# Summing each token's chosen key and value head as a GpSimd tree over a double buffer, in place of a strided VectorE sum

## The chip, the cores and the metric

The kernel runs on one core of a Trainium2 chip. The metric is the device time in microseconds (us) of one execution, lower is better. TensorE (PE in the rows) multiplies matrices into PSUM, VectorE (DVE) and ScalarE (ACT) read PSUM and SBUF, GpSimd (POOL) works on SBUF, and SyncE (SP) issues most of the transfers. All engines run their own list of instructions in order and meet only at semaphores.

## The reference, cut to what matters

The input is one sequence of 2048 tokens of width 256. Three layers follow each other: an attention layer, a gated recurrence, and the attention layer again with the same weights. In an attention layer each token has 16 query heads of 16 elements, but it picks only one of its 16 key heads and one of its 16 value heads:

```python
gating = softmax(x @ W_gate.T)                       # 16 gates per token
indicator = one_hot(argmax(gating), H)
gating_top1 = indicator * max(gating)
qkv = x @ W_qkv.T
k_shared = einsum('bth,bthd->btd', indicator, k)     # the chosen key head, 16 wide
v_shared = einsum('bth,bthd->btd', gating_top1, v)   # the chosen value head, scaled
att = softmax(causal(q @ k_shared.T / sqrt(hd)))
y = att @ v_shared
```

`k_shared` and `v_shared` are sums over the 16 heads, of which all but one are multiplied by zero. These two sums are what the change is about.

## The kernel before, in words

The tokens are four chunks of 512 (`c`), each of four tiles of 128 tokens (`t`). The attention of a layer `l` (0 and 1), a chunk and a group of four heads is a unit, 32 in all. For a unit the kernel first computes all scores once to find the row maxima ("max": a PSUM bank of TensorE scores at L1116, reduced by VectorE at L930, or, for the diagonal blocks, copied by ScalarE at L807, masked by GpSimd at L623 and reduced by VectorE at L936), then computes the scores again ("qk": L1139 and L1142), takes the exponential on ScalarE (L816), masks diagonal blocks on GpSimd (L608, two per diagonal step), and multiplies with the values ("pv": L1152).

Before a chunk's attention comes its preparation, `prepare(l, c)`, of which there are eight: statistics, normalisation, transposes, queries ("q"), gates ("gate", "pick"), and for each of the four tiles "kv" and "choose". "kv" is a TensorE product of all 16 key and 16 value heads into one PSUM bank (L1054), and a VectorE multiplication of that bank with the pick weights into `prod`, 512 elements per token (L894). "choose" is one VectorE reduction over the 16 heads, which reads `prod` with a stride of 16 elements and writes 32 elements of `kv` (L903). VectorE then waits for its own result before its next instruction. "kpack" takes all four tiles of `kv` on ScalarE (L766 and behind), GpSimd computes the rest of the key (L638, L644), ScalarE copies it, and "keys" transposes them on TensorE (L1067). GpSimd also splits the queries (L632, "split"), adds the attention's output to `x_sb` (L614, "fin"), and works in the statistics (L587 to L599) and the recurrence (L653 to L683).

The order of the instructions on every engine is one list, `ORDER`, made by a planner on the host, `weave()` (L155). It keeps a planned time for each engine, takes the duration of each piece from the table `WEIGHT` (L121), and picks among scores, sums, maxima and the side work (preparations and recurrence, whose start is set by `SIDE_WORK`, L111) the one that would be free to start first. In each step the maxima are ranked by how far VectorE's planned time lies ahead. Side work other than "kv", "q" and "skip" is placed behind the planned end of the side work before it (`side_end`). The first preparation, (0,0), stands at the front of the list with no other work beside it. The planner knows of GpSimd's time, but a "pv" behind a diagonal mask is planned at a fixed 900 ns after its scores, however busy GpSimd is.

The PSUM banks of the maxima, preparations and recurrence are a ring of three; TensorE waits before filling a bank until its reader has freed it.

Of the kernel before, what the change touches and what calls it, by code (L numbers as in the profile page):

```python
# [6 lines left out]
D = 256  # L7
H = 16
HD = D // H
S = 128  # L10
P = 128
# [91 lines left out]
def branch(c):  # L103
# [18 lines left out]
    "weights": (300, [("ACT", 400)]), "wgate": (150, [("ACT", 200)]), "bias": (400, [("DVE", 200)]),  # L122
    "stats": (0, [("DVE", 2200), ("POOL", 1500)]), "norm": (0, [("ACT", 2300)]), "turn": (800, [("ACT", 600)]),
    "gate": (2800, [("DVE", 500), ("ACT", 250)]), "pick": (0, [("DVE", 1500)]),
    "kv": (1900, [("DVE", 690)]), "choose": (0, [("DVE", 1020)]), "q": (1900, [("ACT", 600), ("DVE", 690)]),
    "split": (0, [("ACT", 650), ("POOL", 1200)]), "qout": (0, []), "qin": (0, []),
    "kpack": (0, [("ACT", 900), ("POOL", 350)]), "krest": (0, [("ACT", 350), ("POOL", 350)]),
    "keys": (500, [("ACT", 1000)]), "gates": (1900, [("ACT", 690)]), "scan": (0, [("DVE", 1300), ("POOL", 1300)]),
# [187 lines left out]
def macaron_block(nc, x, gamma, beta, w_in, b_in, w_out, b_out, w_skip, b_skip, w_gate, w_qkv, out):  # L316
# [6 lines left out]
    with ctx:  # L323
        def sb(name, shape, dt=f32):
            return ctx.enter_context(nc.sbuf_tensor(name, shape, dt))
# [48 lines left out]
        cand = sb("cand", [P, TC, H])  # L374
        cmx = sb("cmx", [P, TC])
        pick = sb("pick", [P, TC, 2, H])
        prod = sb("prod", [P, 2 * D])
        kv = sb("kv", [P, TC, 2 * HD])

        k_rest = sb("k_rest", [P, TC, HD])  # L380
# [171 lines left out]
        def _(pool):  # L552
# [64 lines left out]
            def diagonal(e):  # L617

                n = DIAG_NO[e]
                if n % 2:  # L620
                    pool.wait_ge(s_ra, FREED[e])
                    d = diag_pair(n // 2)
                    g_.affine_select(out=d, in_=d, compare_op=ALU.is_ge, fill=LOWEST, base=0,  # L623
                                     pattern=[[0, 2 * GH], [-1, P]], channel_multiplier=1).then_inc(s_dm, 1)

            def preparation(e):
                kind, l, c = e[0], e[1], e[2]
                n = prep_no(l, c)
                if kind == "split":
                    b = e[3]  # L630
                    pool.wait_ge(s_q2, NO[e] + 1)
                    g_.tensor_tensor(q_part[:, 2, b, :], q_rest[:, b, :], q_part[:, 1, b, :],  # L632
                                     op=ALU.subtract).then_inc(s_q3, 1)
                elif kind == "kpack":
                    pool.wait_ge(s_k1, n + 1)
                    if n:
                        pool.wait_ge(s_krow, n)
                    g_.tensor_tensor(k_rest[:, :, :], kv[:, :, 0:HD], k_rows[:, 0, :, 0:HD], op=ALU.subtract)\  # L638
                        .then_inc(s_kr, 1)
                elif kind == "krest":  # L640
                    pool.wait_ge(s_kr, n + 1)
                    pool.wait_ge(s_k2, n + 1)
                    rows = k_rows[:, 1, :, :].rearrange("p t (o r) -> p t o r", o=2)[:, :, :, HD:2 * HD]
                    g_.tensor_tensor(rows, k_rest[:, :, :].unsqueeze(2).to_broadcast([P, TC, 2, HD]),  # L644
                                     k_rows[:, 0, :, HD:2 * HD].unsqueeze(2).to_broadcast([P, TC, 2, HD]),
                                     op=ALU.subtract).then_inc(s_krow, 1)
# [38 lines left out]
            for e in ORDER:  # L685
                if e[0] in ("qk", "fin"):
                    attention(e)
                elif e[0] == "stats":
                    stats_of(e)
                    if NO[e] == 0:  # L690
                        constants()
                elif on_diagonal(e):
                    diagonal(e)
                elif e[0] in ("split", "kpack", "krest"):
                    preparation(e)
                elif e[0] in ("bias", "scan", "add") or (e[0] == "norm" and e[1] == 2) \
                        or (e[0] == "gates" and e[2] == 0):
                    recurrence(e)

        @block.scalar  # L700
        def _(act):
# [40 lines left out]
            def preparation(e):  # L742
                kind, l, c = e[0], e[1], e[2]
                n = prep_no(l, c)
                if kind == "gate":
                    act.wait_ge(s_rd, FREED[e])
                    a_.activation(ge[:, :, :], gd[:, :, :], ACT.Exp).then_inc(s_ge, 1)
                elif kind == "q":
                    b = e[3]
                    act.wait_ge(s_fill, filled(e))  # L750
                    if n:
                        act.wait_ge(s_qw[b], 16 * n)
                    a_.activation(q_part[:, 0, b, :], bank_of(e)[:, :], ACT.Copy).then_inc(s_q1, 1)  # L753
                elif kind == "split":
                    b = e[3]
                    act.wait_ge(s_rd, FREED["q", l, c, b])
                    a_.activation(q_part[:, 1, b, :], q_rest[:, b, :], ACT.Copy).then_inc(s_q2, 1)
                elif kind == "kpack":
                    act.wait_ge(s_kv, n + 1)
                    if n == 0:  # L760
                        act.wait_ge(s_const, 1)
                    else:

                        act.wait_ge(s_fill, filled(RING_USERS[max(RING_NO[p] for p in RING_NO
                                                                  if p[0] == "keys" and NO[p] == n - 1)]))
                    a_.activation(v_l[:, l, TC * c:TC * c + TC, 0:HD], kv[:, :, HD:2 * HD], ACT.Copy)  # L766
                    rows = k_rows[:, 1, :, :].rearrange("p t (o r) -> p t o r", o=2)[:, :, :, 0:HD]
                    a_.activation(rows, kv[:, :, 0:HD].unsqueeze(2).to_broadcast([P, TC, 2, HD]), ACT.Copy)
                    rows = k_rows[:, 0, :, :].rearrange("p t (g a d) -> p t g a d", g=4, a=2)
                    a_.activation(rows[:, :, :, 0, :], kv[:, :, 0:HD].unsqueeze(2).to_broadcast([P, TC, 4, HD]),  # L770
                                  ACT.Copy).then_inc(s_k1, 1)
                elif kind == "krest":
                    act.wait_ge(s_kr, n + 1)
                    rows = k_rows[:, 0, :, :].rearrange("p t (g a d) -> p t g a d", g=4, a=2)
                    a_.activation(rows[:, :, :, 1, :], k_rest[:, :, :].unsqueeze(2).to_broadcast([P, TC, 4, HD]),
                                  ACT.Copy).then_inc(s_k2, 1)
# [61 lines left out]
        def _(dve):  # L838
# [3 lines left out]
            def own(ins):  # L842
                n_own[0] += 1
                ins.then_inc(s_dch, 1)
                dve.wait_ge(s_dch, n_own[0])
# [19 lines left out]
            def preparation(e):  # L865
# [24 lines left out]
                elif kind == "kv":  # L890
                    t = e[3]
                    dve.wait_ge(s_fill, filled(e))
                    w = pick[:, t, :, :].rearrange("p a h -> p (a h)")
                    v_.tensor_tensor(prod[:, :].rearrange("p (g d) -> p g d", d=HD),  # L894
                                     bank_of(e)[:, :].rearrange("p (g d) -> p g d", d=HD),
                                     w.unsqueeze(2).to_broadcast([P, 2 * H, HD]), op=ALU.mult)\
                        .then_inc(s_rd, 1)
                elif kind == "choose":
                    t = e[3]
                    dve.wait_ge(s_rd, FREED["kv", l, c, t])  # L900
                    if n and t == 0:
                        dve.wait_ge(s_krow, n)
                    last = v_.tensor_reduce(kv[:, t, :].rearrange("p (a d) -> p a d", a=2),  # L903
                                            prod[:, :].rearrange("p (a h d) -> p a d h", a=2, h=H),
                                            axis=AX, op=ALU.add)
                    if t < TC - 1:
                        own(last)
                    else:
                        last.then_inc(s_kv, 1)
                        dve.wait_ge(s_kv, n + 1)  # L910
                elif kind == "q":
                    b = e[3]
                    dve.wait_ge(s_q1, NO[e] + 1)
                    if n:

                        dve.wait_ge(s_q3, NO[e] - 1)
                    v_.tensor_tensor(q_rest[:, b, :], bank_of(e)[:, :], q_part[:, 0, b, :],  # L917
                                     op=ALU.subtract).then_inc(s_rd, 1)
# [75 lines left out]
            for e in ORDER:  # L994
                if e[0] in ("fold", "join") or (e[0] == "max" and not on_diagonal(e)):
                    maxima(e)
                elif e[0] == "fin":
                    finish(e)
                elif e[0] == "stats":
                    stats_of(e)  # L1000
                elif e[0] in ("gate", "pick", "kv", "choose", "q"):
                    preparation(e)
                elif e[0] in ("bias", "scan", "rec") or (e[0] == "gates" and e[2] == 1):
                    recurrence(e)
# [191 lines left out]
```

## Time and profile before

| what | value |
|---|---|
| median of three runs | 1118.13 us (1112.92 to 1118.16) |
| the profiled execution | 1121.33 us |
| its span, first to last instruction | 1119.6 us |
| mean granted TensorE clock | 0.926 of full speed |
| VectorE busy | 812.9 us, 73% of the span |
| GpSimd busy | 284.8 us, 25% of the span |

The span is what the profile shows instruction by instruction; the time of an execution has 1.7 us around it. Busy time of TensorE is modelled at its end, so that a high share of it does not mean that TensorE works at its peak. A line of a group of instructions gives the line in the kernel, the engine, the operation, the tile written and the tiles read, the shapes, and the count.

### The profile page before, as it was taken

How to read it: one execution, taken by the hardware profiler on the slowest of the kernel's cores; microseconds unless marked ns; L12 is line 12 of the kernel's file. 1: busy time of each engine (PE TensorE's matmuls, PEld its weight loads, DVE VectorE, ACT ScalarE, POOL GpSimd, SP SyncE). 2: the span in 40 equal slices, each digit the busy share in tenths (PEclk: the TensorE clock that was granted, in tenths of full speed). 3: DMA queues.
4: the chain of work that ended last, by engine and by line, in shares of the span. 5: the costliest groups of instructions: out<-in, count | busy, mean ns of one | idle time of the engine just before them, and what ended most of it. 6: DMA issues, size and time to landing. Idle time of an engine off the chain costs nothing.

```text
span 1119.6 us, 20056 instructions
## 1 busy us (share of the span) xinstructions
PE 1027.9 (92%) x7762; PEld 385.0 (34%) x7762; DVE 812.9 (73%) x1441; ACT 713.9 (64%) x1016; POOL 284.8 (25%) x511
## 2 busy tenths in 40 slices
PE   8697898898998997899998999999999999999997
PEld 5334333333233332233333433333333333332322
DVE  3565668778586897679594777886768899999630
ACT  3354357845666674667466754875757777787786
POOL 2244212313223113121113312234222111210314
PEclk8687889998899997899798997998999999999999
DMA  5202011011001100000110011000002000000001
GB/s 161 66 16 71 6 53 29 2 57 30 1 1 43 44 1 1 1 1 1 43 44 1 1 57 30 2 2 19 1 15 71 2 1 20 2 2 1 3 3 38
DMA packets 29966, 26.48 MB, mean 24 GB/s; under 512 B 5664, under 2 KB 29872, under 8 KB 29872
## 3 DMA queue, kind: packets, MB, share of 16 engines
q1 hardware_dynamic: 29056, 24.40, 7.2%
q8 instruction: 62, 1.02, 0.4%
q10 hardware_dynamic: 816, 0.80, 0.2%
q14 instruction: 32, 0.26, 0.1%
HBM read 16.54 MB, written 8.39 MB: 22 GB/s over the span
## 4 chain that ended last, share of the span: by engine, by line
PE 58%; DVE 19%; ACT 8%; issue 4%; POOL 3%; DMA 0%; SPq 0%; POOLq 0%; DVEq 0%; ACTq 0%
PE ps_o L1152 17%; DVE mxp L930 14%; PE ps_x L1116 12%; PE ps_s L1139 8%; PE ps_s L1142 7%; ACT probs L816 4%; PE ps_x L1054 3%; PE ps_x L1059 2%; PE ps_x L1085 2%; PE ps_x L1092 1%; PE ps_x L1125 1%; DVE mxp L936 1%; PE ps_x L1038 1%; PE ps_x L1049 1%; ACT d_sb L807 1%
## 5 line engine op out<-in xcount | busy, mean ns | idle before, releaser
L930 DVE TENSOR_REDUCE mxp<-ps_x 128x1 f32<-128x512 f32 (+2 forms) x960 | 600.1, 682 | 131.5 <-PE ps_x L1116 129.9
L816 ACT ACTIVATE probs<-ps_s 128x1024 f32<-128x1024 f32 (+3 forms) x640 | 545.0, 896 | 222.2 <-PE ps_s L1142 219.6
L1116 PE MATMUL ps_x<-k_tl,q_t 64*128 64x512 bf16 (+2 forms) x1792 | 337.9, 314 | 23.0 <-DVE mxp L930 10.4
L1152 PE MATMUL ps_o<-probs,v_l 128*32 128x512 f32 (+3 forms) x2560 | 310.2, 561 | 9.0 <-POOL probs L608 8.5
L1139 PE MATMUL ps_s<-q_t,k_tl 64*128 64x512 bf16 (+3 forms) x1280 | 288.4, 363 | 13.2 <-ACT probs L816 11.8
L1142 PE MATMUL ps_s<-q_t,k_tl 34*128 34x512 bf16 (+3 forms) x1280 | 286.9, 361 | 0.0
L1116 PEld LDWEIGHTS ps_x<-k_tl,q_t 64*128 64x128 bf16 x1792 | 112.2, 98 | 332.1 <-DVE mxp L930 212.8
L608 POOL TENSOR_SCALAR_AFFINE_SELECT probs<-probs 128x256 f32<-128x256 f32 x256 | 102.2, 407 | 232.6 <-ACT probs L816 229.8
L623 POOL TENSOR_SCALAR_AFFINE_SELECT d_sb<-d_sb 128x1024 f32<-128x1024 f32 x64 | 69.4, 1092 | 260.4 <-ACT d_sb L807 244.3
L1139 PEld LDWEIGHTS ps_s<-q_t,k_tl 64*128 64x128 bf16 x1280 | 81.1, 96 | 110.0 <-ACT probs L816 77.6
L1142 PEld LDWEIGHTS ps_s<-q_t,k_tl 34*128 34x128 bf16 x1280 | 95.5, 97 | 42.1 <-issue 5.4
L807 ACT ACTIVATE d_sb<-ps_x 128x512 f32<-128x512 f32 x128 | 70.6, 606 | 28.7 <-PE ps_x L1116 26.6
L1152 PEld LDWEIGHTS ps_o<-probs,v_l 128*32 128x32 f32 x2560 | 52.3, 109 | 98.0 <-issue 79.7
L936 DVE TENSOR_REDUCE mxp<-d_sb 128x8 f32<-128x1024 f32 x64 | 77.4, 1209 | 0.9 <-POOL d_sb L623 0.9
L1054 PE MATMUL ps_x<-wqkv_t,ut 128*128 128x512 f32 x128 | 63.9, 625 | 1.1 <-DVE prod L894 0.5
L917 DVE TENSOR_TENSOR q_rest<-ps_x,q_part 128x512 f32<-128x512 f32 x16 | 11.1, 691 | 62.9 <-ACT q_part L753 62.9
L614 POOL TENSOR_TENSOR x_sb<-x_sb,y_att 128x256 f32<-128x256 f32 x32 | 24.1, 755 | 95.7 <-DVE y_att L962 95.5
L1059 PE MATMUL ps_x<-ut,wqkv_t 128*128 128x512 f32 x64 | 38.7, 736 | 8.5 <-ACT ut L731 8.5
L958 DVE RECIPROCAL rec<-ps_x 128x16 f32<-128x16 f32 x32 | 8.1, 253 | 45.9 <-PE ps_x L1125 45.8
L753 ACT ACTIVATE q_part<-ps_x 128x512 bf16<-128x512 f32 x16 | 9.6, 597 | 48.4 <-PE ps_x L1059 48.4
L894 DVE TENSOR_TENSOR prod<-ps_x,pick 128x512 f32<-128x512 f32 x32 | 22.1, 691 | 23.5 <-PE ps_x L1054 22.9
L823 ACT ACTIVATE o_sb<-ps_o 128x512 f32<-128x512 f32 x32 | 19.2, 601 | 21.6 <-PE ps_o L1152 21.6
(100 smaller groups left out, 558.5 us busy)
## 6 DMA issues: line engine op xcount, KB each, us to landing
q_t<-q_scratch SPq DMA_DIRECT2D x192, 64.0 KB, 2.2
q_scratch<-q_part SPq DMA_DIRECT2D x16, 384.0 KB, 2.5
x_sb<-in_L_attn_x_dram SPq DMA_DIRECT2D x4, 512.0 KB, 8.3
out_dram<-x_sb SPq DMA_DIRECT2D x4, 512.0 KB, 2.9
q_t<-m_row SPq DMA_DIRECT2D x64, 4.0 KB
wqkv_n<-in_L_ffn_W_qkv_dram ACTq DMA_DIRECT2D x1, 768.0 KB, 6.7
w_in_sb<-in_L_attn_W_in_dram SPq DMA_DIRECT2D x1, 384.0 KB, 5.7
w_skip_sb<-in_L_attn_W_skip_dram SPq DMA_DIRECT2D x1, 256.0 KB, 5.2
```

The source lines that it names most:

```text
L608: g_.affine_select(out=pr, in_=pr, compare_op=ALU.is_ge, fill=0.0, base=0, pattern=[[0, 2], [1, P]], channel_multiplier=-1).then_inc(s_msk, 1)
L623: g_.affine_select(out=d, in_=d, compare_op=ALU.is_ge, fill=LOWEST, base=0, pattern=[[0, 2 * GH], [-1, P]], channel_multiplier=1).then_inc ...
L807: a_.activation(d_sb[:, n % DIAG_BUFS, :], bank_of(e)[:, :], ACT.Copy).then_inc(s_ra, 1)
L816: a_.activation(probs[:, s % NB, 2 * hp:2 * hp + 2, P * i:QW], ps_s[hp][:, :, P * i:QW], ACT.Exp, scale=SCALE).then_inc(s_exp, 1)
L930: v_.tensor_reduce(mxp[:, heads[0] % 2, h0:h1, tiles[0]:tiles[-1] + 1:i_step, slot], bank_of(e)[:, :].rearrange("p (h i k) -> p h i k", i= ...
L936: v_.tensor_reduce(mxp[:, :, :, 2 * i2:2 * i2 + 2, 2].rearrange("p o h i -> p (o h) i"), diag_pair(2 * v + i2).rearrange("p (x i) k -> p x ...
L1054: last = mm(bank[:, :], ut[:, dc, t * P:(t + 1) * P], wqkv_t[:, dc, D:3 * D], start=dc == 0, stop=dc == DC - 1)
L1059: last = mm(bank[:, :], wqkv_t[:, dc, b * P:(b + 1) * P], ut[:, dc, :], start=dc == 0, stop=dc == DC - 1)
L1116: last = mm(bank[:, col:col + w], q_rows(0, ROWS_A, c, g, hh, i * P, P), k_cols(0, ROWS_A, hh, l, key // P, w), start=True, stop=True)
L1139: mm(ps_s[hp][:, hh, P * i:QW], k_cols(0, ROWS_A, hh, l, kt, P), q_rows(0, ROWS_A, c, g, 2 * hp + hh, P * i, QW - P * i), start=True, stop ...
L1142: last = mm(ps_s[hp][:, hh, P * i:QW], k_cols(1, ROWS_B, hh, l, kt, P), q_rows(1, ROWS_B, c, g, 2 * hp + hh, P * i, QW - P * i), start=Fal ...
L1152: last = mm(ps_o[VW * hh:VW * hh + VW, P * i:QW], v_l[:, l, kt, :], probs[:, s % NB, hh, P * i:QW], start=j == 0, stop=j == key_tiles(c) - 1)
```

## The change

"choose" moves from VectorE to GpSimd. There it is a tree of four additions in place: 8 heads onto 8, 4 onto 4, 2 onto 2, and the last into `kv`, each for key and value together (256, 128, 64 and 32 elements per partition). The first three each wait for their own end before the next. `prod` becomes two buffers, by the parity of the tile. VectorE's multiplication now waits until the "choose" two before it has ended (`s_kv` counts every "choose" now, not every fourth), and ScalarE's "kpack" waits for all four. The reduction, and VectorE's waits around it, are gone. In the planner's table "choose" goes from 1020 ns on VectorE to 1900 ns on GpSimd, so `ORDER` is planned anew from there.

```diff
-    "kv": (1900, [("DVE", 690)]), "choose": (0, [("DVE", 1020)]), "q": (1900, [("ACT", 600), ("DVE", 690)]),
+    "kv": (1900, [("DVE", 690)]), "choose": (0, [("POOL", 1900)]), "q": (1900, [("ACT", 600), ("DVE", 690)]),
...
-        prod = sb("prod", [P, 2 * D])
+        prod = sb("prod", [P, 2, 2 * D])
...
+            def choose(e):
+                _, l, c, t = e
+                n = prep_no(l, c)
+                pool.wait_ge(s_rd, FREED["kv", l, c, t])
+                if n and t == 0:
+                    pool.wait_ge(s_krow, n)
+                parts = prod[:, t % 2, :].rearrange("p (a h d) -> p a h d", a=2, h=H)
+                w = H // 2
+                while w > 1:
+                    own(g_.tensor_tensor(parts[:, :, 0:w, :], parts[:, :, 0:w, :], parts[:, :, w:2 * w, :], op=ALU.add))
+                    w //= 2
+                g_.tensor_tensor(kv[:, t, :].rearrange("p (a d) -> p a d", a=2), parts[:, :, 0, :], parts[:, :, 1, :],
+                                 op=ALU.add).then_inc(s_kv, 1)
...
-                    act.wait_ge(s_kv, n + 1)
+                    act.wait_ge(s_kv, TC * (n + 1))
...
-                    v_.tensor_tensor(prod[:, :].rearrange("p (g d) -> p g d", d=HD),
+                    if NO[e] >= 2:
+                        dve.wait_ge(s_kv, NO[e] - 1)
+                    v_.tensor_tensor(prod[:, t % 2, :].rearrange("p (g d) -> p g d", d=HD),
...
-                elif kind == "choose":
-                    t = e[3]
-                    dve.wait_ge(s_rd, FREED["kv", l, c, t])
-                    if n and t == 0:
-                        dve.wait_ge(s_krow, n)
-                    last = v_.tensor_reduce(kv[:, t, :].rearrange("p (a d) -> p a d", a=2),
-                                            prod[:, :].rearrange("p (a h d) -> p a d h", a=2, h=H),
-                                            axis=AX, op=ALU.add)
-                    if t < TC - 1:
-                        own(last)
-                    else:
-                        last.then_inc(s_kv, 1)
-                        dve.wait_ge(s_kv, n + 1)
```

## Rows read from the trace of the kernel before

**Rows 1.** The page: busy time by engine (part 1), the chain by engine (part 4)
```profile
PE 1027.9 (92%) x7762; PEld 385.0 (34%) x7762; DVE 812.9 (73%) x1441; ACT 713.9 (64%) x1016; POOL 284.8 (25%) x511
...
PE 58%; DVE 19%; ACT 8%; issue 4%; POOL 3%; DMA 0%; SPq 0%; POOLq 0%; DVEq 0%; ACTq 0%
```

**Rows 2.** Waits of all engines: total us, times, longest
```profile
PEld ps_x L1116 <- DVE mxp L930: 212.8, 415, 1.6
...
PE ps_o L1152 <- POOL probs L608: 8.5, 4, 4.7
```

**Rows 3.** Groups by form, VectorE: busy us, mean ns, idle before, releasers
```profile
L930 DVE TENSOR_REDUCE mxp<-ps_x 128x1 f32<-128x512 f32 x768 | 478.0, 681 | 68.9 <-PE ps_x L1116 67.6
...
L903 DVE TENSOR_REDUCE kv<-prod 128x32 f32<-128x512 f32 x32 | 32.4, 1013 | 0.3
L894 DVE TENSOR_TENSOR prod<-ps_x,pick 128x512 f32<-128x512 f32 x32 | 22.1, 691 | 23.5 <-PE ps_x L1054 22.9
```

**Rows 4.** The chain, shares by line, in 232:262, 354:384, 554:580, 652:678, 826:856
```profile
by line: PE ps_x L1054 19.5%; PE ps_o L1152 13.2%; DVE mxp L930 12.3%; PE ps_x L1116 11.3%; DVE prod L894 5.9%; PE ps_x L1059 5.7%; DMA q_t<-m_row 5.7%; PE ps_s L1142 5.1%; PE ps_s L1139 5.1%; DVE kv L903 3.4%; issue 2.9%; PE ps_x L1125 2.1
...
by line: DVE mxp L930 32.8%; DVE kv L903 13.0%; PE ps_x L1054 12.8%; DVE prod L894 6.9%; PE ps_o L1152 6.6%; PE ps_x L1059 5.8%; PE ps_s L1139 5.5%; issue 5.3%; PE ps_s L1142 4.9%; PE ps_x L1116 4.7%; ACT q_part L753 2.0%; DVE rec L958 0.9%
...
by line: PE ps_x L1054 33.5%; PE ps_o L1152 20.5%; PE ps_x L1116 15.1%; PE ps_s L1139 9.0%; PE ps_s L1142 8.5%; PE ps_x L1059 6.6%; ACT probs L816 6.3%; DVE prod L894 2.7%; issue 1.9%; DVEq L892 0.1%
...
by line: PE ps_x L1054 29.6%; PE ps_o L1152 20.8%; PE ps_x L1116 11.1%; PE ps_s L1139 7.7%; PE ps_s L1142 6.8%; PE ps_x L1059 6.6%; DVE prod L894 5.4%; DVE mxp L930 5.0%; DVE kv L903 4.0%; ACT probs L816 4.0%; issue 1.2%; DVEq L892 0.2%
...
by line: DVE mxp L930 21.6%; PE ps_x L1054 12.8%; PE ps_o L1152 12.3%; DVE mxp L936 7.5%; PE ps_x L1116 7.1%; DVE prod L894 6.6%; DVE kv L903 6.5%; issue 6.2%; ACT probs L816 5.9%; PE ps_x L1059 5.7%; PE ps_s L1139 4.6%; PE ps_s L1142 3.4%;
```

**Rows 5.** Groups by form, GpSimd, of 512 elements down to 4
```profile
L614 POOL TENSOR_TENSOR x_sb<-x_sb,y_att 128x256 f32<-128x256 f32 x32 | 24.1, 755 | 95.7 <-DVE y_att L962 95.5
L632 POOL TENSOR_TENSOR q_part<-q_rest,q_part 128x512 bf16<-128x512 f32 x16 | 18.5, 1156 | 50.9 <-ACT q_part L757 50.2
...
L644 POOL TENSOR_TENSOR k_rows<-k_rest,k_rows 128x128 bf16<-128x128 f32 x8 | 3.4, 426 | 10.0 <-ACT k_rows L775 10.0
...
L638 POOL TENSOR_TENSOR k_rest<-kv,k_rows 128x64 f32<-128x64 f32 x8 | 2.4, 304 | 48.9 <-ACT k_rows L770 48.9
L598 POOL TENSOR_TENSOR shift<-mv,rstd 128x4 f32<-128x4 f32 x12 | 2.4, 199 | 0.9
...
L653 POOL TENSOR_TENSOR b_out_r<-b_out_r,b_skip_r 128x256 f32<-128x256 f32 x1 | 0.7, 726 | 0.0
```

**Rows 6.** Timeline of 0:45, the first preparation: start us, us, engine line
```profile
9.54 0.20 POOL L598 TENSOR_TENSOR shift<-mv,rstd 128x4 f32<-128x4 f32 x1
9.83 0.24 POOL L599 TENSOR_SCALAR shift<-shift 128x4 f32<-128x4 f32 x1
...
23.46 0.69 DVE L894 TENSOR_TENSOR prod<-ps_x,pick 128x512 f32<-128x512 f32 x1
...
24.15 5.31 PE L1054 MATMUL ps_x<-wqkv_t,ut 128*128 128x512 f32 x12
...
26.41 1.16 POOL L632 TENSOR_TENSOR q_part<-q_rest,q_part 128x512 bf16<-128x512 f32 x1 [3.06 <-ACT q_part L757]
...
30.90 1.00 DVE L903 TENSOR_REDUCE kv<-prod 128x32 f32<-128x512 f32 x1
...
31.94 0.26 ACT L766 ACTIVATE v_l<-kv 128x64 f32<-128x64 f32 x1 [5.61 <-DVE kv L903]
...
36.47 1.01 PE L1116 MATMUL ps_x<-k_tl,q_t 64*128 64x128 bf16 x12 [1.21 <-ACT k_tl L734]
```

**Rows 7.** Timeline of GpSimd in 354:384, the preparation (1,0), last mask and first key rest
```profile
363.85 0.41 POOL L608 TENSOR_SCALAR_AFFINE_SELECT probs<-probs 128x256 f32<-128x256 f32 x1
380.82 0.30 POOL L638 TENSOR_TENSOR k_rest<-kv,k_rows 128x64 f32<-128x64 f32 x1 [16.56 <-ACT k_rows L770]
```

**Rows 8.** Masks of the exponentials (L608): duration ns min/median/max, first and last start
```profile
L608 POOL TENSOR_SCALAR_AFFINE_SELECT probs<-probs x256: 402/406/416, 56.6 to 1112.3; 128x256 f32<-128x256 f32 x128
```

More of the change, by code:

```diff
@@ L693, in _ @@
                     diagonal(e)
+                elif e[0] == "choose":
+                    choose(e)
                 elif e[0] in ("split", "kpack", "krest"):
@@ L1000, in _ @@
                     stats_of(e)
-                elif e[0] in ("gate", "pick", "kv", "choose", "q"):
+                elif e[0] in ("gate", "pick", "kv", "q"):
                     preparation(e)
```

## The prediction

> **What bounds the kernel now.** I read the page first. TensorE is shown busy for 92% of the span, VectorE for 73%, GpSimd for 25%; the chain of work that ended last runs 58% over TensorE and 19% over VectorE [rows 1]. So VectorE is the second limit, and it is one only in places. The waits say where: TensorE's weight loads for the maxima waited 415 times, 212.8 us in total, for VectorE's reduction to free a bank [rows 2]. The reader should see that this is a loop of two engines over three banks, in which now one and now the other is late. An instruction taken from VectorE is worth its time only where VectorE is the late one.
>
> The reduction that the change removes runs 32 times at 1013 ns, 32.4 us in all [rows 3]. It is dear for its 512 elements: the maxima's reduction, also over 512, takes 681 ns [rows 3].
>
> To see where it counts I asked for the chain in each stretch that holds a preparation's four tiles. It carries L903 in four of the eight preparations, and in the last of these stretches as in the second VectorE's maxima are the chain's largest item too [rows 4]. In the stretch of (1,1) it isn't on the chain at all; TensorE's own work is [rows 4]. In the stretches of (0,1) and (0,2) I found none either, and ahead of 91 us the chain view shows nothing, so the first preparation has to be read from the timeline.
>
> **The change part by part.**
>
> *The reduction leaves VectorE.* By the chain it is worth 3.4% of 30 us, 13.0% of 30, 4.0% of 26 and 6.5% of 30 [rows 4]: 1.0 + 3.9 + 1.0 + 2.0 = **7.9 us**. The bounds: nothing, if TensorE is late everywhere once VectorE is a little lighter (in those stretches TensorE's lines stand right behind); and 32.4 us [rows 3], if the planner packs the maxima into every gap. I take 7.9, the reading nearest to the work itself.
>
> *The tree on GpSimd.* Four additions of 256, 128, 64 and 32 elements. 256 elements take 726 to 755 ns, 128 took 426 (with half-size output; on the line between 304 and 726 it would be 445), 64 take 304, and 32 lie between 199 (4 elements) and 304, say 250 [rows 5]. That is 1.74 us. Each of the first three waits for its own end; in the timeline such a handover is 0.09 us, from 9.54 + 0.20 to 9.83 [rows 6], so 0.27 more: **2.0 us for a tree**, 64 us for 32, GpSimd going from 284.8 to about 349 us, 31% of the span. The bounds of one tree: 1.7 us with no handovers, and 2.9 with every level at the next larger row (1156 + 726 + 426 + 304, and 0.27) [rows 5].
>
> The Trainium skill (GPSIMD Engine Reference, Performance versus the Vector engine) puts an addition of two inputs at about 2.6 cycles of 1.2 GHz per element: 480 elements would take 1.04 us, an estimate from that page without any start cost. By it the tree would be near the planner's 1.9 or below; by the rows each of the four instructions carries some 190 ns of its own [rows 5], and the rows decide.
>
> *Beside what it lies.* In (1,0) GpSimd is idle for 16.56 us before it gets the keys' rest [rows 7]; two trees and their products fit in there. So the 64 us cost nothing where the last tile's sum isn't urgent, and the cover is GpSimd's 75% of idle time. Without that cover each tree would cost its 2.0 us.
>
> *The first preparation.* Here nothing lies beside it and every link counts. Before, VectorE does product and sum in turn, the last sum ends at 31.90, ScalarE takes it at 31.94 and the first maxima start at 36.47, released by the keys [rows 6]. After, the products follow TensorE: its twelve matmuls of tiles 1 to 3 run evenly from 24.15 to 29.46 [rows 6], tile 2's to 27.7, so the fourth product ends near 30.2. But GpSimd has four trees and a query split (1.16 us, not before 26.41) in its list [rows 6]. The first product ends at 24.15, so tree 0 runs 24.2 to 26.2, the split 26.4 to 27.6, then trees 1, 2, 3 end at 29.6, 31.7 and 33.8. "kpack" starts at 33.8 instead of 31.94: **1.9 us lost**. With a tree of 1.7 it is 0.9, with 2.9 it is 5.1. Nothing takes this back, as the keys release the first maxima.
>
> *The other preparations' tail.* "kpack" now waits for a tree of 2.0 instead of a sum of 1.0. Where VectorE is loaded (the stretches of rows 4) the product itself comes earlier by the sums no longer ahead of it, and this cancels. In (0,1), where VectorE idles, it does not: I put **0.5 us**, between 0 and 2.0 (the whole tree).
>
> *The new waits.* The product waits for the tree two before it. Queued behind it on VectorE are the maxima, and TensorE waits for those. In steady preparations the tiles lie several us apart; in (0,0) tree 0 has ended at 26.2 before product 2 can start at 27.7, and tree 1 at 29.6 just as product 3 becomes ready. I take nothing; with a tree of 2.9 tree 1 ends at 31.2 and product 3 comes 1.7 us late, which is inside the 5.1 above. GpSimd now waits for VectorE's product with its own masks queued behind: 256 masks of 0.41 us [rows 8], and TensorE's products with the values wait for them. Today that wait is 8.5 us in 4 cases [rows 2], so most masks have slack. I add **1 us**, half a case; at worst, see the second rival. No DMA is added or moved past another; the query loads keep their places on SP.
>
> *The new order.* The list is planned anew from the second preparation on. That has no row: from 0 it can go either way. I take 0 and let it widen the range by about 6 us on each side, three of today's mask waits (8.5/4 = 2.1 us each [rows 2]).
>
> *The sum:* −7.9 + 1.9 + 0.5 + 1.0 = −4.5 us against the profiled execution, 1121.33, which gives 1116.8. That execution stands 3.2 us above the median of the three runs, so the median would be 1113.6; I say **1113**.
>
> A measurement of this kernel can tell about 0.5% (5.6 us) from no change; below, faster means under 1112.5 and slower over 1123.7.
>
> **The rivals.**
>
> *VectorE's relief is worth more than its chain share (faster).* The maxima are ranked by VectorE's planned time, and 1.02 us less per tile lets them move up, also after the preparation. For it: the 212.8 us of waits for VectorE [rows 2], and that L930 is the largest item in two of the stretches [rows 4]. Against: in the others TensorE's lines lead. If half of the 32.4 us comes back, less 3.4 for the costs above, it is −12.8: 1105. If all, 1089.
>
> *GpSimd's queue becomes the wait (slower).* Place: the diagonal steps of (0,1), (0,2) and (1,0). A tree stands in GpSimd's list ahead of a mask, its product is late because VectorE has a backlog of maxima, and the mask waits for product and tree; TensorE stands at the "pv". The planner doesn't see this, as it plans that "pv" at a fixed 900 ns. Price: a mask wait averages 2.1 us now and the longest took 4.7 [rows 2]. If 8 of the 32 trees hit at 2.1 us, it is 17 us, and with the sum above +12: 1130. It decides when more than about 5 trees hit (5 × 2.1 = 10, which turns the sum positive beyond noise). Against: only 4 of 256 masks are late today, and GpSimd has long idle stretches [rows 2, 7]. The Trainium skill (GPSIMD Engine Reference, When to use GPSIMD) speaks for this rival: it keeps sums along the free dimension on VectorE and calls GpSimd about twice as slow for two inputs. The rows agree on the price (2.0 us for 1.0), but not that it must be paid on the path.
>
> *The change does nothing much (same).* If TensorE takes over as the late one wherever L903 was on the chain, the gain is 0 and 3.4 us of cost are left: 1121.5. For it: the stretch of (1,1), where L903 is absent and the chain is TensorE's [rows 4].
>
> **How the numbers follow.** The forecast itself, within 5.6 us of no change, 0.27; nothing much, 0.15 (both "same", 0.42). Larger relief, with the part of the forecast's own spread under 1112.5, 0.38. GpSimd's queue or an unlucky order, 0.20. The range reaches from a bit more than the half-relief case (1101) to short of the queue rival's full price (1127); it leaves out all of the relief coming back and the queue hit eight times.
>
> **What would show it.** VectorE's busy time falls by 32 us to about 781, the products' mean stays near 691 ns, GpSimd's rises to about 349 with trees of 1.7 to 2.0 us. The first "kpack" copy (L766) starts near 33.8 instead of 31.94. The wait of "pv" for the masks stays under 15 us; if it is over 20, the queue rival holds. VectorE's share of the chain falls by about a point. The prediction is wrong if the waits of TensorE for L930 fall by tens of us (relief), or if the product waits for GpSimd.

## The result, and the profile after

The changed kernel takes 1130.81 us (median of four, 1124.37 to 1131.51) against 1117.32 in the same session: a ratio of **1.0111**, interval 1.0083 to 1.0139. By the ratio it is 12 us slower, and it lies outside the forecast's range of 1101 to 1127. Ratios here and below leave out executions more than 1.5% above the fastest of their kernel, which is one of e10_best's six and no other.

The page of the changed kernel, parts 1 and 2 (busy time, then the span in 40 slices of 28.2 us, tenths of full clock):

```profile
PE 1047.7 (93%) x7762; PEld 386.8 (34%) x7762; DVE 783.8 (69%) x1409; ACT 714.7 (63%) x1016; POOL 338.5 (30%) x639
...
PEclk7678877988999996899799999999999976999999
```

VectorE gave up 29 us and GpSimd took 54 (812.9 and 284.8 before, [rows 1]). That is the change doing what it says. But the clock has a dip near the end, at slices 33 and 34, that the kernel before doesn't have.

The trees, as groups by form of the changed kernel (busy us, mean ns, idle before):

```profile
L636 POOL TENSOR_TENSOR prod<-prod 128x256 f32<-128x256 f32 x32 | 23.2, 725 | 43.7 <-DVE prod L914 43.7
...
L636 POOL TENSOR_TENSOR prod<-prod 128x128 f32<-128x128 f32 x32 | 14.6, 455 | 2.5
L636 POOL TENSOR_TENSOR prod<-prod 128x64 f32<-128x64 f32 x32 | 10.2, 319 | 2.5
...
L638 POOL TENSOR_TENSOR kv<-prod 128x32 f32<-128x32 f32 x32 | 8.0, 251 | 2.5
```

725 + 455 + 319 + 251 = 1750 ns, and 7.5 us over 96 handovers is 0.08 each: 2.0 us for a tree, as forecast from [rows 5]. The estimate by the Trainium skill (GPSIMD Engine Reference, Performance versus the Vector engine) had been 1.04 us. Per element the trace agrees with that page, (725 − 251)/224 = 2.1 ns against 2.2; what the estimate leaves out are some 180 ns that each of the four instructions takes besides (251 − 32 × 2.1).

The two waits of [rows 2] answer with these, of the changed kernel:

```profile
PEld ps_x L1123 <- DVE mxp L937: 218.0, 436, 1.0
...
PE ps_o L1159 <- POOL probs L608: 9.6, 6, 4.7
```

The wait for masks went from 8.5 to 9.6 us: GpSimd's masks are not where the time went. The wait for VectorE didn't fall, though VectorE does 29 us less; 20.4 us of the 218.0 lie in one stretch, to which we come now.

**Where it went.** ScalarE evicts each unit's output once (`o_sb`), so these 32 instructions are milestones. Set side by side, the changed kernel is 6.7 us late at unit 0, swings between 15.6 us late (unit 14) and 8.5 ahead, and is 7.8 us ahead at unit 23. Then this, the timeline of the kernel before:

```profile
922.61 0.60 ACT L823 ACTIVATE o_sb<-ps_o 128x512 f32<-128x512 f32 x1 [1.32 <-PE ps_o L1152]
965.65 0.60 ACT L823 ACTIVATE o_sb<-ps_o 128x512 f32<-128x512 f32 x1
```

and of the changed kernel, from unit 23's eviction to unit 24's:

```profile
914.84 0.60 ACT L840 ACTIVATE o_sb<-ps_o 128x512 f32<-128x512 f32 x1
...
918.84 25.12 PE L1123 MATMUL ps_x<-k_tl,q_t 64*128 64x512 bf16 x51 [0.21 <-DVE mxp L937]
...
943.89 1.11 PE L1132 MATMUL ps_x<-ident,o_sb 128*128 128x128 f32 x4
...
982.83 0.60 ACT L840 ACTIVATE o_sb<-ps_o 128x512 f32<-128x512 f32 x1
```

43 us became 68, so that the changed kernel is now 17.2 us late; 7.4 of these come back in the units behind, and 9.8 are left at the end. For 25.12 us TensorE issues nothing but matmuls of maxima, 51 of them, at VectorE's pace, while ScalarE's exponentials stand still. What ends it is the transpose of unit 23's output (L1132), which had been ready since 915.4. The same 26 us in windows, the changed kernel first (busy us and count of PE, PEld, DVE, ACT, POOL; clock; DMA share and GB/s):

```profile
918.00:944.00 26.00, 25.73 (x58) 5.27 (x58) 25.89 (x46) 1.90 (x6) 1.17 (x3) 0.51 0.00 0
```

```profile
918.00:944.00 26.00, 23.91 (x212) 8.30 (x211) 23.36 (x38) 18.45 (x25) 5.77 (x11) 1.00 0.07 22
```

VectorE is busy for 25.89 of the 26 us, so it is what holds the stretch back. PE is "busy" for 25.7 of 26 us with 58 matmuls, where the kernel before does 212 in 23.9. The clock granted in this stretch is 0.51, nearly all at the lower level of 1.2 GHz, against 1.00.

The cause stands in the planner, in code that the change doesn't touch (`t` is when a piece could start by the plan, `now` is TensorE's planned time; the lowest wait is taken, and among equal waits the lowest rank):

```python
elif e[0] == "fin":
    rank = -1e6 if t <= now else 1e5
...
found.append((max(0.0, t - now), rank, work))
```

The output transpose "fin" needs a bank of the same ring of three as the maxima. While VectorE is behind, no bank is free "now", for either; both have the same planned wait (414 or 630 ns in most of these choices), and then "fin" loses by rank, each time. The sums behind it in its list ("pv" of the next unit) can't go, and after four steps the scores can't either. So the planner lays maxima only, until a diagonal maximum comes, whose bank ScalarE reads and frees early. In the order made with the old table this doesn't happen (its longest run of maxima and their follow-up work, without any other piece, is 20 list entries); with 1900 ns on GpSimd it happens once, 44 entries ahead of unit 23's "fin".

### The profile page after: what moved, and what is told of

Its sections match the earlier page's. It is cut to its first block and busy times, and to the rows that moved or that the text cites. A ratio compares the mean times of both kernels' runs of the same rounds, so it can differ in the third digit from the quotient of the medians.

```text
span 1129.4 us, 20139 instructions
## 1 busy us (share of the span) xinstructions
PE 1047.7 (93%) x7762; PEld 386.8 (34%) x7762; DVE 783.8 (69%) x1409; ACT 714.7 (63%) x1016; POOL 338.5 (30%) x639
## 3 DMA queue, kind: packets, MB, share of 16 engines
q8 instruction: 62, 1.02, 0.4%
## 5 line engine op out<-in xcount | busy, mean ns | idle before, releaser
L1123 PE MATMUL ps_x<-k_tl,q_t 64*128 64x128 bf16 (+2 forms) x1792 | 348.6, 320 | 19.4 <-DVE mxp L937 8.3
L1146 PE MATMUL ps_s<-q_t,k_tl 64*128 64x512 bf16 (+3 forms) x1280 | 284.2, 361 | 8.9 <-ACT probs L833 7.6
L1149 PE MATMUL ps_s<-q_t,k_tl 34*128 34x512 bf16 (+3 forms) x1280 | 281.4, 358 | 0.0
L1123 PEld LDWEIGHTS ps_x<-k_tl,q_t 64*128 64x128 bf16 x1792 | 113.5, 98 | 331.8 <-DVE mxp L937 218.0
L608 POOL TENSOR_SCALAR_AFFINE_SELECT probs<-probs 128x256 f32<-128x256 f32 x256 | 102.0, 406 | 303.3 <-ACT probs L833 300.7
L1061 PE MATMUL ps_x<-wqkv_t,ut 128*128 128x512 f32 x128 | 68.2, 661 | 0.2
L636 POOL TENSOR_TENSOR prod<-prod 128x256 f32<-128x256 f32 (+2 forms) x96 | 48.0, 500 | 48.7 <-DVE prod L914 43.7
```

What stands on the lines that cost most here:

```text
L608: g_.affine_select(out=pr, in_=pr, compare_op=ALU.is_ge, fill=0.0, base=0, pattern=[[0, 2], [1, P]], channel_multiplier=-1).then_inc(s_msk, 1)
L636: own(g_.tensor_tensor(parts[:, :, 0:w, :], parts[:, :, 0:w, :], parts[:, :, w:2 * w, :], op=ALU.add))
L1061: last = mm(bank[:, :], ut[:, dc, t * P:(t + 1) * P], wqkv_t[:, dc, D:3 * D], start=dc == 0, stop=dc == DC - 1)
L1123: last = mm(bank[:, col:col + w], q_rows(0, ROWS_A, c, g, hh, i * P, P), k_cols(0, ROWS_A, hh, l, key // P, w), start=True, stop=True)
L1146: mm(ps_s[hp][:, hh, P * i:QW], k_cols(0, ROWS_A, hh, l, kt, P), q_rows(0, ROWS_A, c, g, 2 * hp + hh, P * i, QW - P * i), start=True, stop ...
L1149: last = mm(ps_s[hp][:, hh, P * i:QW], k_cols(1, ROWS_B, hh, l, kt, P), q_rows(1, ROWS_B, c, g, 2 * hp + hh, P * i, QW - P * i), start=Fal ...
```

## The experiments

Theory A: the loss is this accident of the new order. Theory B: the loss is GpSimd's queue. Ratios are to the kernel before on the same chip, each with its 95% interval; 1% is 11 us. The runs are spread over several chips, so two runs are compared by their ratios, and the difference of two ratios carries both intervals.

**e1_old_order.** The move, with the old order:

```diff
-    "choose": (0, [("POOL", 1900)])
+    "choose": (0, [("DVE", 1020)])
```

> The sums are done on GpSimd as in the changed kernel, but the planner's table still says 1020 ns on VectorE, so the order of all instructions is that of the kernel before. Theory A (the loss is the new order: one stretch of 25 us in which TensorE does maxima only because the output transpose of unit 23 is put off) expects 1111 to 1118 us: the start's 2 us lost, some of the 7.9 us won. Theory B (the loss is GpSimd's queue: trees that come late or stand before masks) expects 1125 us or more, as the work on GpSimd is the same.

1.0003 (0.9981 to 1.0025). Theory B falls: the same work on GpSimd in the old order costs nothing and wins nothing that can be told, within 2.5 us either way.

**e2_new_order.** The kernel before, its table set to 1900 ns on GpSimd, its sums left on VectorE.

> The kernel before, its sums still on VectorE, with the order planned for 1900 ns on GpSimd. Theory A expects the 25 us stretch to be there and no relief on VectorE: 1130 to 1145 us. Theory B expects no loss from the order: 1112 to 1120 us.

1.0148 (1.0130 to 1.0166). The order alone costs 16.5 us, with no tree anywhere. Its timeline has the same stretch:

```profile
920.05 24.52 PE L1116 MATMUL ps_x<-k_tl,q_t 64*128 64x512 bf16 x50 [0.21 <-DVE mxp L930]
```

The changed kernel differs from this run only in where the sums are done, and lies at 1.0111 against 1.0148: in this order the move is worth some 4 us, just clear of the two intervals. Even the masks' wait is longer without the trees, 11.1 us against 9.6:

```profile
PE ps_o L1152 <- POOL probs L608: 11.1, 5, 5.5
```

**e3_fin23.** The changed kernel, one piece not put off. The list is the same up to that point, with the work behind it planned anew:

```diff
-                rank = -1e6 if t <= now else 1e5
+                rank = -1e6 if t <= now or e[1] == 23 else 1e5
```

> The changed kernel, with one rule of the planner set aside for one piece: the output transpose of unit 23 is taken as soon as it is no later than the other choices, instead of last. The order is the same up to there. Theory A expects the stretch near 918 us to be gone and 1103 to 1115 us (1130.8 less 25, plus up to 7 that the shorter tail gave back). Theory B expects no more than 5 us off: 1125 us or more.

1107.84 us, 0.9913 (0.9877 to 0.9949): some 22 us less than the changed kernel, with one piece exempt from one rule. Unit 23's eviction starts at 908.91 and its transpose follows 1.0 us later, in the timeline of e3_fin23:

```profile
908.91 0.60 ACT L840 ACTIVATE o_sb<-ps_o 128x512 f32<-128x512 f32 x1
...
909.92 0.66 PE L1132 MATMUL ps_x<-ident,o_sb 128*128 128x128 f32 x4
```

**e4_table1700.** 1700 in place of 1900.

> The changed kernel with 1700 instead of 1900 ns in the planner's table. Its order holds two long runs of maxima (43 and 46 instructions, ahead of the output transposes of units 10 and 22), against one of 44 in the changed kernel. Theory A expects about 20 us more than the changed kernel, 1145 to 1160 us. Theory B expects the changed kernel's time within 5 us.

1.0256 (1.0198 to 1.0314), from two executions only, 1141.97 and 1152.54 us. The first of its two stretches, in its timeline:

```profile
412.44 23.92 PE L1123 MATMUL ps_x<-k_tl,q_t 64*128 64x512 bf16 x49 [0.21 <-DVE mxp L937]
```

**e5_table2000.** 2000 in place of 1900, the tree's measured time.

> The changed kernel with 2000 ns, what a tree takes on the chip, instead of 1900 ns in the planner's table. The planner's order then has no run of maxima longer than 23, as with the old table. Theory A (the loss is the put-off output transpose) expects 1104 to 1114 us, near the run with unit 23's transpose put right (1107.8). Theory B' (that run was good because of something else in its order) expects no relation to it.

0.9903 (0.9869 to 0.9937), 1105.12 us. A change of 5% in one entry of the table, and no change in the work, is worth some 23 us.

**e6_fin_all.** The changed kernel, no output transpose put off:

```diff
-                rank = -1e6 if t <= now else 1e5
+                rank = -1e6
```

> The changed kernel with the planner's rule set aside for all output transposes: they are taken as soon as no other choice is earlier. Theory A expects 1102 to 1112 us. If putting off a transpose is useful elsewhere, this is slower than the run with unit 23 alone by a few us.

1099.38 us, **0.9856** (0.9815 to 0.9896), better than both kernels.

**e7_before_fin_all.** The same edit in the kernel before.

> The control: the kernel before, sums on VectorE, with the same rule set aside for all output transposes. Its order holds no long run of maxima to begin with. If the gain of the mended kernels came from the rule alone, this gains as much, 1105 to 1110 us. If it takes VectorE's relief as well (theory A with a relief that only a new order can use), this is 1115 to 1127 us.

1.0087 (1.0057 to 1.0117), 1128.92 us, a little above the expected time: the rule isn't a gain in itself. It makes another order, and on the old table a worse one.

**e11_new_order_fin23.** The order of e3_fin23, sums on VectorE (the edits of e2 and e3 on the kernel before).

> The kernel before, sums on VectorE as before, with the mended new order of the run e3_fin23 (table at 1900 ns on GpSimd, unit 23's transpose not put off). It tells order from relief: e3_fin23 differs from it only in where the sums are done. If the whole gain is a better order, this is 1106 to 1112 us, like e3_fin23. If the new order is only good because VectorE is relieved, it is 1113 to 1122 us.

0.9917 (0.9883 to 0.9952), the same as e3_fin23's 0.9913. In this order, too, no worth of the move shows, though the two intervals leave room for 5 us either way. The gain over the kernel before is there without the move: it comes from the order.

**r18_fin_all_vector.** The order of e6_fin_all, sums on VectorE.

> The order of e6_fin_all (table at 1900 ns on GpSimd, no output transpose put off) with the sums on VectorE as before the change. If the order is the whole gain, as in the pair e3_fin23 and e11_new_order_fin23, 1098 to 1106 us, the same as e6_fin_all. If this order leans on VectorE's relief, 1107 us or more.

0.9972 (0.9956 to 0.9987), 1115.4 us in a spread of 1112.8 to 1117.2, against 1097.6 to 1107.1 for e6_fin_all. Here the move is worth 1.2%, some 13 us. So its worth depends on the order: nothing that shows in two of them, some 4 us in that of e2_new_order, 13 us here (the interval of this difference is about 5 us on each side). What this order does with the relief wasn't found.

**Why the move alone is worth nothing.** The next four take apart the relief of VectorE and the trees, all in the old order.

**r13_relief_only.** Each tree cut to its last addition, which leaves out 14 of the 16 heads:

```diff
-                w = H // 2
+                w = 1
                 while w > 1:
```

> e1_old_order with each tree cut to its last addition (heads 0 and 1 only, so that 14 of the 16 products are left out of each sum): 0.25 us instead of 2.0. VectorE is relieved as in e1_old_order, and the trees' latency is gone. If the relief is worth the 7.9 us of the prediction and the trees take it back, this is 1107 to 1112 us (start 1 to 2 us earlier too). If the relief is worth nothing in itself, 1114 to 1118 us.

0.9961 (0.9944 to 0.9978): 4.4 us won. GpSimd is busy for 292.0 us, VectorE for 783.9. So the relief has a worth, 2.5 to 6.3 us by the interval, about half of the forecast's. The full trees of e1_old_order take it back: from 0.9961 to 1.0003 is 4.7 us, with some 3 us of error on each side.

**e9_trees_twice.** Trees made twice in seven of eight preparations (n is the preparation's number):

```diff
+                w = H // 2
+                while n and w:
+                    own(g_.tensor_tensor(twice[:, :, 0:w, :], parts[:, :, 0:w, :], parts[:, :, w:2 * w, :], op=ALU.add))
+                    w //= 2
```

> The run with the old order, e1_old_order, with every tree but the first preparation's four made twice (once into a scratch tile that nobody reads): 28 more trees, 57 us more of GpSimd. If GpSimd's queue costs nothing as long as it is idle most of the time (theory A), this is 1115 to 1123 us; if trees on GpSimd stand in the way of masks (theory B), another 10 us or more, over 1128.

1.0214 (1.0172 to 1.0257): 24 us for 28 trees. Theory A's guess that GpSimd's idle time covers a tree anywhere is wrong. The waits say which engine pays. ScalarE's first copy of the sums (`v_l`), of e1_old_order:

```profile
ACT v_l L783 <- POOL kv L638: 12.9, 6, 7.1
```

of e9_trees_twice:

```profile
ACT v_l L788 <- POOL kv L643: 32.5, 8, 7.1
```

of the kernel before:

```profile
ACT v_l L766 <- DVE kv L903: 6.2, 2, 5.6
```

ScalarE takes its list in order, and behind the copy stand exponentials. Theory B had named 1128 us or more for this run, so its queue isn't out of the matter yet; the next two tell last trees from others.

**r14_twice_first_two.** As e9, with `while n and t < 2 and w`.

> e9_trees_twice with only the trees of tiles 0 and 1 made twice: 14 extra trees, 28 us of GpSimd. If the tail's latency is what costs (ScalarE waiting for the last sum), these cost nothing: 1116 to 1122 us. If GpSimd's time as such costs, half of the 27 us: about 1131.

1.0062 (1.0041 to 1.0084), about 7 us over e1_old_order. ScalarE's wait is 13.0 us, unchanged. That isn't nothing, and less than the half that GpSimd's time as such would give. What did rise is the wait for masks, of e1_old_order and then of r14_twice_first_two:

```profile
PE ps_o L1159 <- POOL probs L608: 7.3, 4, 5.1
```

```profile
PE ps_o L1164 <- POOL probs L609: 12.6, 6, 5.5
```

So GpSimd's queue, theory B, does act once the early trees are twice as long: 5.3 us more of waiting, most of it in two places that had none before (at 373 and 570 us) and in one that had 1.0 us (at 80). With single trees it doesn't: in e1_old_order this wait is 7.3 us against 8.5 in the kernel before.

**r15_twice_last.** As e9, with `while n and t == 3 and w`.

> e9_trees_twice with only the last tree of each preparation made twice: 7 extra trees, 14 us of GpSimd. If the tail's latency costs, each adds its 2 us to ScalarE's wait, 7 x 2 = 14 us at most, 1124 to 1134 us. If GpSimd's time as such costs, a quarter of the 27: about 1125, and less than the run with tiles 0 and 1.

1.0143 (1.0098 to 1.0189), about 16 us over e1_old_order for 7 trees, with half of r14's extra work. ScalarE's wait, of r15_twice_last:

```profile
ACT v_l L788 <- POOL kv L643: 26.1, 8, 7.1
```

Each extra last tree costs about its whole length, 16/7 = 2.2 us, with an error of some 0.8; ScalarE's wait rose by 13.2/7 = 1.9 for each. Each of the first two costs 7/14 = 0.5. What costs most is the latency of a preparation's last sum.

**e12_one_buffer.** e3_fin23 with one buffer of products.

> The run e3_fin23 with one buffer of products instead of two, same order: each multiplication waits for the tree just before it. In the first preparation products and trees then take turns (0.7 + 2.0 us each): its last sum comes about 2 us later. In the others the tiles lie apart. I expect 0 to 4 us more than e3_fin23, 1106 to 1114 us.

0.9929 (0.9904 to 0.9954), against 0.9913. The intervals overlap: what the second buffer brings in time is below what was measured. It isn't idle, though. With one buffer VectorE's products wait for the trees, of e12_one_buffer:

```profile
DVE prod L914 <- POOL kv L638: 23.4, 12, 3.4
```

In e3_fin23 this is 1.1 us in one case. 22 us more of waiting on VectorE show up in the time as nothing that could be told.

**e8_first_on_vector.** e3_fin23 with the first preparation's sums on VectorE:

```diff
-                elif e[0] == "choose":
+                elif e[0] == "choose" and e[1:3] != (0, 0):
```

with the old reduction kept on VectorE for that case.

> The run with unit 23's transpose put right, but the four sums of the first preparation are left on VectorE, with the same order. In the run with the old order the first copy of the sums starts at 33.76 us against 31.94 before; here it should start near 32 us. If the first preparation's latency is on the path to the end, the time is 1.5 to 2 us less than 1107.8; if something later hides it, the same.

0.9842 (0.9823 to 0.9860), 0.7% better than e3_fin23 and more than the edit can give. So both went side by side again.

**r16_fin23_again.**

> The same kernel as e3_fin23, as the base for the next run: 1104 to 1113 us, in two clusters as before.

**r17_first_again.**

> The same kernel as e8_first_on_vector. If the first preparation's 2 us reach the end, it is about 2 us faster than the run beside it; if the fifth unit hides them, equal within 0.3%; the 0.7% between the earlier calls would then be their two clusters and not the edit.

0.9933 (0.9905 to 0.9961) and 0.9932 (0.9907 to 0.9957): equal, but the difference carries an error of 4 us on each side, so the 2 us looked for can't be ruled out. The profiles don't settle it. Those of e3 and e8 agree to 0.3 us from unit 5's eviction to unit 26's, as if the loss were hidden by then; those of r16 and r17, the same two kernels, lie 2.3 us apart at unit 5 and 5.1 at unit 7. Whether the first preparation's loss reaches the end stays open.

**e10_best.** e6_fin_all with the first preparation on VectorE.

> Both that helped together: the planner's rule set aside for all output transposes, and the first preparation's four sums left on VectorE. If the two add up, 1094 to 1099 us; if the first preparation's latency is hidden further on, as its units from the fifth on suggest, 1098 to 1101 us, the same as e6_fin_all.

0.9811 (0.9757 to 0.9864), with executions spread from 1089.1 to 1107.9 us: not told apart from e6_fin_all. Both beat both kernels.

## Why the prediction was wrong

- **"The new order … has no row … I take 0 and let it widen the range by about 6 us on each side."** This is the step that failed. Between e1_old_order and the changed kernel only the order differs, and it costs 12 us; between the kernel before and e2_new_order again only the order, 16.5 us. Neither sign nor size could be had by counting instructions. The bound of 6 us had been taken from mask waits, which have nothing to do with how the planner can go wrong. What the runs showed in its place is a stretch of 25 us of maxima ahead of unit 23's output transpose, which goes with that one rule for that one piece (e3_fin23). The planner's code was there to read: a piece that loses every tie and has all later sums queued behind it.
- **The relief, 7.9 us.** Too large. All the sums gone and almost no trees gave 4.4 us (r13), the first preparation's shorter start included. This is the larger size that was wrong in the sum for the old order: the costs were put at 3.4 us and came out at some 4.7 (r13 to e1_old_order), while the relief was put at 7.9. The chain's share of an instruction says how long it lay on the chain, not what the chain loses without it. The stretch with the largest share, 3.9 us in (1,0), shows it: e1_old_order is 4.8 us late at unit 9's eviction and 5.0 at unit 10's, on either side of that stretch, and r13_relief_only 2.6 and 2.9, so nothing came back there.
- **The tree, 2.0 us.** Right, part by part.
- **The first preparation, 1.9 us, "kpack" at 33.8.** Right in place: in e1_old_order the copy starts at 33.76. "Nothing takes this back" is neither borne out nor refuted: no loss showed in r16 and r17, to within 4 us.
- **The other tails, 0.5 us, and "this cancels".** Too small. ScalarE's wait for the last tree rose by 6.7 us in e1_old_order, of which 1.5 in the first preparation. The longest waits behind that one are 2.11 us in (0,3), 1.50 in (1,2) and 1.02 in (1,0), and these are stretches where the sums left the chain and the earlier product was to cancel the longer tree. I had GpSimd's masks as what is queued behind a tree, and passed over the copy on ScalarE with the exponentials behind it.
- **GpSimd's queue as the rival on the slower side.** The time was near its 1130, but by another mechanism. That this rival's chance, 0.20, also held "an unlucky order" names the right place by luck, without a mechanism or a price of its own. The masks' wait rose by 1.1 us over the kernel before, and fell by 1.5 where only the trees differ (e2_new_order to the changed kernel). The Trainium skill's page that speaks for that rival (GPSIMD Engine Reference, When to use GPSIMD) is right on the price, 2.0 us for 1.0, and the price isn't what made the kernel slower.
- **"The change does nothing much."** That is what the move does in the old order, 1.0003, though by gain and cost cancelling (r13), not by a gain of 0.

## What to carry to other kernels

When an edit changes a cost in a table from which an order is planned, measure it twice: with the old order and with the new one. Here the two differ by 12 us, more than what the edit itself does in three of the four orders in which it was tried, and 100 ns in the table are worth more than 20 us. When work moves to a slower engine, ask first who waits for its last piece and what is queued behind that waiter; the slower engine's idle time covers the other pieces far better than that one. And a planner that breaks ties against a piece on which others depend should have a limit on how long that piece can lose; the longest run of one kind of work in the order shows such a case before any run does.

## What the hardware showed that was not expected

Executions of one kernel on one chip spread more than one median shows: e11_new_order_fin23 gave 1102.1 to 1103.6 four times, 1107.4 once and 1114.6 to 1115.8 five times. Part of this may be the start, though not all: a profiled execution of e12_one_buffer with the lower clock at the start belongs to the lower group of its times. The first 28 us were granted 0.88 of the full clock in the profile of the kernel before, and 0.76 in the one of the changed kernel, with nearly the same TensorE work (windows of the kernel before, then of the changed one):

```profile
0.00:28.00 28.00, 23.28 (x99) 16.13 (x100) 8.50 (x22) 8.97 (x19) 7.18 (x37) 0.88 0.53 161
```

```profile
0.00:28.00 28.00, 23.29 (x90) 16.83 (x91) 5.53 (x18) 7.64 (x17) 7.21 (x39) 0.76 0.50 155
```

By unit 0's eviction the second was 6.7 us behind. e3_fin23, the same kernel up to unit 22, was granted 0.88 and was 0.5 us behind there, and the 6 us between these two were still there at unit 22 (8.3 us ahead of the kernel before against 14.2).

Dips come in the middle, too. From unit 13's eviction to unit 14's e1_old_order and r13_relief_only both take 58.4 us, and the kernel before takes 63.0. That looks like the relief at work and need not be: the kernel before was granted 0.50 at 550 us and again at 600 us, and e1_old_order 1.00 both times (the kernel before, then e1_old_order):

```profile
550.00:555.00 5.00, 4.92 (x15) 2.20 (x16) 3.70 (x10) 1.94 (x2) 1.54 (x3) 0.50 0.44 134
600.00:605.00 5.00, 4.33 (x21) 1.98 (x21) 1.28 (x4) 3.39 (x6) 2.36 (x1) 0.50 0.01 3
```

```profile
550.00:555.00 5.00, 4.28 (x37) 1.57 (x32) 5.00 (x9) 2.72 (x6) 1.16 (x1) 1.00 0.16 53
600.00:605.00 5.00, 2.88 (x31) 1.56 (x33) 1.36 (x4) 4.68 (x9) 2.37 (x1) 1.00 0.01 3
```

So comparing two single profiles stage by stage carries an error of some 6 us from the start alone, half of what was looked for here, and dips further on can add to it. The stretch of 25 us stands far above that.
